# GpSimd issues its row scatters one by one, behind units of the cross attention and gates of expert blocks

## The chip, the cores and the metric

The kernel runs on one core of a Trainium2 chip. The metric is device time in microseconds; lower is better. The core has TensorE (PE, matrix products into PSUM), VectorE (DVE), ScalarE (ACT), GpSimd (POOL) and SyncE (SP), which run on their own and meet through semaphores, and 16 DMA engines that all queues share.

## What is computed

Two decoder layers on `x` (4 batches of 256 rows, 256 wide, float32), each with self attention, cross attention and a feed-forward part. The part around the change is the end of layer 1: its cross attention and its mixture of experts.

```python
x = x + _L1_attn_ref(_layernorm(x), w_qkv, b_qkv, w_out, b_out)
x = x + _L1_xattn_ref(_layernorm(x), ctx_512, Wq, Wkv_expand, Wout)      # 16 heads, causal, 256 x 256
x = x + _L1_ffn_ref(_layernorm(x), gate_weight, w_gate, w_up, w_down)
...
logits = x @ gate_weight.T                        # 28 experts
topk_w, topk_idx = jax.lax.top_k(softmax(logits), 6)
topk_w = topk_w / (topk_w.sum(-1, keepdims=True) + 1e-20)
# for every expert: h = silu(x @ wg) * (x @ wu);  y += w_tok * (h @ wd)     wg, wu: 256 x 176, wd: 176 x 256
```

## The kernel before, in words

Every engine works through a fixed list of pieces. `plan()` writes the lists; for layer 1 they are spelled out by hand in `ORDERS`, one string per engine, and a piece `sc.1.2` means the call `sc(1, 2)` in that engine's block. An engine executes its list strictly in order, and waits inside a piece stop everything behind it on that engine.

**Cross attention.** 32 units, `x` unit i being half of a head group of batch i // 8. For a unit TensorE makes the scores (`xs`), VectorE two negated maxima (L2026 and L2027, which count up semaphore `x_nm`), ScalarE the exponentials (L2556, L2557) in place of the scores, TensorE transposes them (`xt`, L851), ScalarE copies these back, and after every second unit comes the product with the values (`xpv`), which VectorE copies out (L2039). Three units are in flight, in three pairs of PSUM banks. Among the units lie the projections and the ends (`xe_...`) of each batch.

**Routing.** For batch b (256 rows): VectorE normalizes the rows (`rt_xh`, L2073; GpSimd does the power -0.5 for it, L2671), TensorE turns them and multiplies with the gate weights (`rt_tr`, `rt_g`), VectorE takes the maximum (L2080, semaphore `rt_m`), ScalarE the exponentials, VectorE the six best (`rt_k`), and `rt_p` gives each of the 256 x 6 row copies its place in the DRAM table `xg`, which has room for 1024 rows per expert (L2127 writes the places, semaphore `pos`). GpSimd then issues 12 indirect DMAs per batch: each takes 128 rows of 272 floats and scatters them to `xg` (L2738). These are the row scatters of this case. The places and rows are double buffered, so `rt_xh` of batch b waits for all 12 of batch b - 2.

**Block tables.** `mn`, `mc`, `ms` make, from the counts, tables of which half blocks (64 rows of one expert) come next. `ms.0` (after batches 0 and 1) fills expert pairs 0 to 4, `ms.1` pairs 5 to 10, `ms.2` the rest up to 30 (`FIRST = (0, 5, 11, NPAIR)`).

**Expert pairs.** There are 62 blocks of 128 rows (two half blocks each), in 31 pairs. SyncE's piece `ld(q)` loads the rows of pair q + 3 from `xg` (L784) and weights of pair q + 2 (L799). Where pair p starts a new table it waits first for all row scatters of the batches it rests on:

```python
if p in FIRST:
    for b in range(turn(p) + 2):
        e.wait_ge(sem(f"xg{b}"), 16 * 12)
```

The buffer of a block is free when the block 12 places before it has been scaled. ScalarE copies the block's expert weights (`wc`, L2278, `ws<-W_all`), TensorE transposes the rows (`et`), multiplies with gate and up weights (`eu`), ScalarE takes silu (L2632, semaphore `sg`), VectorE multiplies (L2216 to L2219), TensorE transposes (`eh`) and multiplies down (`ed`), VectorE scales the result with the routing weight (`ed`, L2240 and L2242), and GpSimd adds the 128 rows to one of two DRAM tables, `y0` or `y1`, with an indirect DMA that accumulates (`ed` of GpSimd, L2757). An add waits for the landing of the one before it on the same table, blocks alternate between the two, and VectorE has 10 result buffers. At the end SyncE reads the tables back and VectorE adds them to `x`.

GpSimd has, besides the scatters and adds, only small work in this part: the power steps (L2671) and a fill of zeros (`hm`).

Of the kernel before, what the change touches and what calls it, by code (L numbers as in the profile page):

```python
# [52 lines left out]
def half(h):  # L53
# [57 lines left out]
    "POOL": (  # L111
# [37 lines left out]
class Plan:  # L149
# [7 lines left out]
    def add(self, name, *args, banks=(), told=True, only=None):  # L157
        self.seq.append((name, args, only))
        mine = []
        for b in banks:  # L160
            mine.append((b, self.k[b], self.f[b]))
            if name != "w":
                self.k[b] += 1
                self.f[b] += told
        if only in (None, "PE"):
            self.fills[(name, *args)] = mine
# [18 lines left out]
def plan():  # L185
    p = Plan()
    add = p.add
# [142 lines left out]
    def experts():  # L330
        for q in range(5, NPAIR + 1):
            if q + 2 < NPAIR:
                add("ld", q)
            add("ed", q - 1, banks=[5, 6])
            if q < NPAIR:
                add("eh", q, banks=[4])
            if q + 2 < NPAIR:
                add("et", q + 2, banks=[q % 2])
            for j in (2 * q + 2, 2 * q + 3):
                if j < NB:  # L340
                    add("eu", j, banks=[2 + j % 2])
            if q + 2 < NPAIR:
                add("wc", q + 2)
        add("out")

    experts()
    return p


def program(nc, D):  # L350
    ctx = ExitStack()
    with ctx:
# [3 lines left out]
        def sem(name):  # L356
            if name not in sems:
                sems[name] = ctx.enter_context(nc.semaphore(name))
            return sems[name]
# [9 lines left out]
        def fills(name, *args):  # L369
            return [Fill(B[b], full[b], free[b], k, f) for b, k, f in P.fills[(name, *args)]]  # L370

        def fill(name, *args):
            return fills(name, *args)[0]
# [104 lines left out]
        at = bqkv_base  # L478
# [10 lines left out]
        at = fgu_base  # L489
        U = parts("U", 8, 256)  # L490
        at = r2_base + 4 * c2.at
# [5 lines left out]
        at = fwo_base + 4 * c3.at  # L497
        OT.append(parts("OT1", 256))
        assert at <= fwo_base + 4 * 4096
        at = fwd_base  # L500
# [50 lines left out]
        sg = [cm(176) for _ in range(2)]  # L551
# [58 lines left out]
        posi = [c1(12).bitcast(I32), pos2[:, :].bitcast(I32)]  # L610
# [230 lines left out]
        def _(e):  # L841
# [478 lines left out]
            def u_pv(i):  # L1320
                b, _, rh = unit(i)
                u = fill("upv", i)
                if i % 4 == 1:
                    w = fill("vtr", b, 1)
                    e.wait_ge(w.free, w.k + 1)
                for w in fills("ut", i - 1) + fills("ut", i):
                    e.wait_ge(w.free, w.k + 1)
                room(u)
                for r in range(4):
                    for j in range(4):  # L1330
                        a = mm(u.t[32 * j:32 * j + 32, r * 128:r * 128 + 128], va4[b % 2][:, 4 * rh + r, 32 * j:32 * j + 32],
                               PTu[slot_t("u", i - 1 + j // 2)][:, 4 * (j % 2) + r, :], True, True)
                a.then_inc(u.full, 1)
# [259 lines left out]
        def _(e):  # L1593
# [398 lines left out]
            def u_pv(i):  # L1992
                b, _, rh = unit(i)
                u = fill("upv", i)
                if b >= 2:
                    e.wait_ge(sem("scrw"), 16 * (b - 1))
                e.wait_ge(u.full, u.f + 1)
                o = O4[b % 2].rearrange("p (m x e) -> p e m x", m=4, e=2)[:, rh]
                e.tensor_copy(o, u.t[:, :].rearrange("p (m x) -> p m x", m=4)).then_inc(u.free, 1)
# [647 lines left out]
        def _(e):  # L2647
# [25 lines left out]
            def ln(tiles):  # L2673
                for t in tiles:
                    rstd((rs[:, t:t + 1], rs[:, t:t + 1]))
# [51 lines left out]
                e.tensor_tensor(Pu[m], Pu[m], rcu[m].rearrange("p (g o) -> p g o", o=1).to_broadcast([128, 8, 128]),  # L2727
                                ALU.mult).then_inc(sem("un"), 1)

            def sc(b, part):  # L2730
                xr = xrs[b % 2]
                if b == 0:
                    e.wait_ge(sem("init"), 16 * (NE + 1 + NY))
                e.wait_ge(sem("pos"), b + 1)
                e.wait_ge(sem("xr"), 3 * b + 3)
                e.wait_ge(sem("xh_rt"), 2 * b + 2)
                for i in range(3 * part, 3 * part + 3):
                    e.indirect_dma_start(out=D["xg"][:, :], out_offset=bass.IndirectOffsetOnAxis(ap=posi[b % 2][:, i:i + 1], axis=0),  # L2738
                                         in_=xr[:, i // 6, :], in_offset=None).then_inc(sem(f"xg{b}"), 16)


            def hm():
# [18 lines left out]
            def pair(b):  # L2761
# [3 lines left out]
                    "x0_bn": x0_bn,  # L2765
                    "x0_stat2": pair, "rest": rest, "rms1": lambda: rms(1), "rms2": lambda: rms(2),
                    "l1_stat": lambda t0, t1: ln(range(t0, t1)), "l1_init": l1_init, "un": un, "xp_stat": pair,
                    "rt_stat": pair, "sc": sc, "hm": hm, "ed": ed}
            for name, args, only in P.seq:
                if name in mine and only in (None, "POOL"):  # L2770
                    mine[name](*args)
# [119 lines left out]
```

## Time and profile before

| | |
|---|---|
| median of 3 runs | 814.88 us (807.21 to 815.64) |
| profiled execution, its own time | 808.85 us |
| its span, first to last instruction | 807.0 us |
| mean granted clock of TensorE | 0.916 |
| TensorE busy | 690.9 us, 86% |
| VectorE, ScalarE, GpSimd busy | 476.7, 376.4, 286.2 us |

The profile is one execution. Times count from the start of its span. A row of the timeline or of a line's group ends with the idle time of the engine before it and, after an arrow, what ended it; "issue" means nothing that the profile shows, "remote" a semaphore update from a source that it can't name.

### The profile page before, as it was taken

How to read it: one execution, taken by the hardware profiler on the slowest of the kernel's cores; microseconds unless marked ns; L12 is line 12 of the kernel's file. 1: busy time of each engine (PE TensorE's matmuls, PEld its weight loads, DVE VectorE, ACT ScalarE, POOL GpSimd, SP SyncE). 2: the span in 40 equal slices, each digit the busy share in tenths (PEclk: the TensorE clock that was granted, in tenths of full speed). 3: DMA queues.
4: the chain of work that ended last, by engine and by line, in shares of the span. 5: the costliest groups of instructions: out<-in, count | busy, mean ns of one | idle time of the engine just before them, and what ended most of it. 6: DMA issues, size and time to landing. Idle time of an engine off the chain costs nothing.

```text
span 807.0 us, 15683 instructions
## 1 busy us (share of the span) xinstructions
PE 690.9 (86%) x5129; PEld 472.3 (59%) x5136; DVE 476.7 (59%) x1413; ACT 376.4 (47%) x1026; POOL 286.2 (35%) x279
## 2 busy tenths in 40 slices
PE   8898999999879988798988999698648699999960
PEld 6666687777535766687756766466424355554530
DVE  2567669788867545546664756345425366665555
ACT  2464556555411502545657367436323256555520
POOL 3043544454410002212310402412445656566550
PEclk9999999999999999979997999858568799999985
DMA  8999999002150034313000019603334578778767
GB/s 330 296 349 350 349 348 379 7 1 76 59 215 18 0 124 126 113 37 105 27 28 1 1 31 404 239 22 145 103 114 103 104 129 148 144 143 148 135 106 235
DMA packets 86077, 116.89 MB, mean 145 GB/s; under 512 B 8364, under 2 KB 77293, under 8 KB 84974
## 3 DMA queue, kind: packets, MB, share of 16 engines
q1 hardware_dynamic: 70140, 97.71, 37.4%
q0 software_dynamic: 11168, 14.75, 10.7%
q10 hardware_dynamic: 4690, 3.43, 1.5%
q8 instruction: 43, 0.70, 0.4%
q14 instruction: 36, 0.29, 0.1%
HBM read 59.82 MB, written 56.04 MB: 144 GB/s over the span
## 4 chain that ended last, share of the span: by engine, by line
PE 35%; issue 5%; DVE 5%; another core or an unknown queue 3%; ACT 3%; DMA 2%; ACTq 1%; POOL 0%; SPq 0%; DVEq 0%; POOLq 0%
PE PS L843 28%; PE PS L851 8%; DMA y<-fwd 1%; ACTq L2609 1%; ACT ws L2278 1%; DVE few L1974 1%; ACT R L2496 1%; DMA W_all<-y 1%; DVE few L2027 0%; DMA y<-late,fwd 0%; DVE few L2026 0%; DVE R L1981 0%; DVE R L2102 0%; ACT R L2557 0%
## 5 line engine op out<-in xcount | busy, mean ns | idle before, releaser
L843 PE MATMUL PS<-R 32*128 32x128 f32 (+11 forms) x1048 | 138.1, 376 | 9.9 <-DVE R L2102 2.1
L843 PE MATMUL PS<-W_all,fgu 128*64 x372 | 113.7, 453 | 11.5 <-DVE fgu L2227 7.5
L843 PE MATMUL PS<-ws,fgu 128*64 128x352 f32 (+1 forms) x372 | 114.0, 454 | 0.0
L843 PEld LDWEIGHTS PS<-R 32*128 32x128 f32 (+5 forms) x1048 | 86.6, 196 | 43.5 <-issue 25.3
L2278 ACT ACTIVATE R<-PS 128x512 f32<-128x512 f32 (+5 forms) x136 | 67.6, 546 | 44.8 <-PE PS L851 31.9
L851 PE MATMUL PS<-ident,R 128*128 128x128 f32 (+1 forms) x504 | 75.7, 291 | 11.9 <-POOL R L2727 3.9
L843 PEld LDWEIGHTS PS<-W_all,fgu 128*64 128x64 f32 x372 | 49.4, 142 | 60.2 <-issue 27.5
L851 PEld LDWEIGHTS PS<-ident,R 128*128 128x128 f32 (+1 forms) x504 | 58.8, 150 | 33.6 <-issue 19.7
L2278 ACT ACTIVATE ws<-W_all 128x960 f32 x62 | 58.8, 996 | 25.3 <-issue 25.3
L2671 POOL TENSOR_TENSOR rs<-rs,mh 128x1 f32<-128x1 f32 x48 | 26.8, 561 | 111.5 <-DVE rs L1611 111.2
L2727 POOL TENSOR_TENSOR R<-R 128x1024 f32<-128x1024 f32 x16 | 30.3, 1900 | 100.1 <-DVE R L1983 100.1
L2681 POOL TENSOR_TENSOR R<-R 128x512 f32<-128x512 f32 x44 | 44.9, 1041 | 56.8 <-DVE R L1710 56.8
L2757 POOL DMA_INDIRECT y<-late,fwd x30 | 46.6, 1553 | 30.6 <-DVE late L2242 12.4
L2360 ACT ACTIVATE R<-PS,R 128x256 f32<-128x256 f32 x88 | 40.4, 473 | 28.9 <-DVE R L1702 28.9
L1695 DVE TENSOR_REDUCE R<-PS 128x2 f32<-128x512 f32 x64 | 41.1, 683 | 20.9 <-PE PS L843 20.5
L843 PEld LDWEIGHTS PS<-ws,fgu 128*64 128x64 f32 x372 | 49.4, 142 | 0.5 <-issue 0.5
L2757 POOL DMA_INDIRECT y<-fwd x20 | 31.3, 1565 | 40.1 <-DVE fwd L2242 20.4
L2632 ACT ACTIVATE fwd<-PS 128x176 f32<-128x176 f32 x62 | 19.5, 317 | 54.9 <-PE PS L843 26.1
L2496 ACT ACTIVATE R<-PS,few 128x128 f32<-128x128 f32 x128 | 34.6, 396 | 16.8 <-DVE few L1974 16.7
L843 PE MATMUL PS<-negm,identb 128*128 128x512 bf16 (+1 forms) x146 | 33.9, 343 | 4.4 <-DVE fwo L1758 1.6
L2278 ACT ACTIVATE xT<-PS 128x256 f32<-128x256 f32 (+1 forms) x32 | 13.4, 441 | 47.7 <-PE PS L851 44.3
L2026 DVE TENSOR_REDUCE few<-PS 128x2 f32<-128x256 f32 x32 | 13.5, 423 | 36.6 <-PE PS L843 26.4
(342 smaller groups left out, 1570.0 us busy)
## 6 DMA issues: line engine op xcount, KB each, us to landing
xg<-zrow SPq DMA_DIRECT2D x28, 1088.0 KB, 12.4
W_all<-in_wgu SPq DMA_DIRECT2D x2, 3360.0 KB
xh<-xg SPq DMA_DIRECT2D x74, 68.0 KB
y<-zrow SPq DMA_DIRECT2D x2, 2304.0 KB, 16.1
W_all<-in_wgu SPq DMA_DIRECT2D x1, 4320.0 KB
R<-in_wqkv SPq DMA_DIRECT2D x1, 4096.0 KB, 21.2
scrq<-bqkv SPq DMA_DIRECT2D x12, 256.0 KB, 2.9
R<-scrq SPq DMA_DIRECT2D x12, 256.0 KB, 3.0
```

Of the source, the lines that this page charges most:

```text
L843: return e.matmul(out, l, r, start=start, stop=stop, skip_group_check=True)
L851: return e.transpose(out, a, ident[:, :] if idt is None else idt)
L1695: own.mark(e.tensor_reduce(mx[s][:, :, hh], us[hh].t[:, :].rearrange("p (q k) -> p q k", q=2), X, ALU.max))
L2026: e.tensor_reduce(m[:, 0:2], PS[:, b0:b0 + 2, 0:128], X, ALU.max, negate=True).then_inc(sem("x_nm"), 1)
L2278: return e.activation(out, a, ACT.Copy)
L2360: a = e.activation(Pr[2 * (j % 3) + hh][:, qc, :], us[hh].t[:, qc * 256:qc * 256 + 256], ACT.Exp, bias=nb[s][:, qc, hh:hh + 1], scale=SA, ...
L2496: a = e.activation(Pu[m][:, g, :], us[jj].t[:, r * 128:r * 128 + 128], ACT.Exp, bias=mxx[m][:, g:g + 1], scale=1.0)
L2632: e.activation(sg[j % 2], u.t[:, 0:176], ACT.Silu).then_inc(sem("sg"), 1)
L2671: e.tensor_tensor(v[1], v[0], mh[:, 0:1], ALU.pow).then_inc(sem("rstd"), 1)
L2681: e.tensor_tensor(p, p, rc[j % 2][:, :, hh:hh + 1].to_broadcast([128, 2, 256]), ALU.mult).then_inc(sem("norm"), 1)
L2727: e.tensor_tensor(Pu[m], Pu[m], rcu[m].rearrange("p (g o) -> p g o", o=1).to_broadcast([128, 8, 128]), ALU.mult).then_inc(sem("un"), 1)
L2757: e.indirect_dma_start(out=D[f"y{y}"][0:to, :], out_offset=bass.IndirectOffsetOnAxis(ap=toi[j % NYS][rows, :], axis=0), in_=ys[j % NYS][ro ...
```

## The change

The piece `sc(b, part)` issued three scatters; now `sc(b, i)` issues one, and GpSimd's list holds 48 such pieces in place of 16. New pieces that only wait stand between them: `at(i)` waits until VectorE has taken the maxima of unit i, `top(b)` until it has taken the router's maxima of batch b, `pv(i)` until it has copied the value product of unit i, and `sg(j)` until ScalarE has the silu of block j. The adds of result rows (`ed`) keep their order and now lie between the scatters of batch 3, of which the last five are issued in the loop of the experts, behind pairs 4 to 6. The lists of the other engines are as they were.

```diff
--- before.py
+++ after.py
@@ -110,9 +110,11 @@
         "wc.4 et.5 eu.8 eu.9 wc.5 et.6 eu.10 eu.11 wc.6 "),
     "POOL": (
         "l1_stat.2.4 l1_stat.4.6 l1_stat.6.8 l1_init un.0 un.1 un.2 un.3 un.4 un.5 un.6 un.7 un.8 xp_stat.0 "
-        "un.9 un.10 xp_stat.1 un.11 un.12 un.13 xp_stat.2 un.14 rt_stat.0 un.15 xp_stat.3 sc.0.0 rt_stat.1 "
-        "sc.0.1 sc.0.2 sc.0.3 sc.1.0 rt_stat.2 sc.1.1 sc.1.2 sc.1.3 sc.2.0 sc.2.1 rt_stat.3 hm sc.2.2 sc.2.3 "
-        "ed.0 sc.3.0 sc.3.1 ed.1 sc.3.2 sc.3.3 ed.2 ed.3 "),
+        "un.9 un.10 xp_stat.1 un.11 un.12 un.13 xp_stat.2 un.14 rt_stat.0 un.15 xp_stat.3 at.17 sc.0.0 at.18 sc.0.1 at.19 sc.0.2 at.20 sc.0.3 rt_stat.1 at.21 sc.0.4 at.22 sc.0.5 at.23 "
+        "sc.0.6 sc.0.7 at.24 sc.0.8 sc.0.9 at.25 sc.0.10 sc.0.11 at.27 sc.1.0 at.28 sc.1.1 sc.1.2 at.29 sc.1.3 sc.1.4 "
+        "rt_stat.2 at.30 sc.1.5 sc.1.6 at.31 sc.1.7 sc.1.8 top.2 sc.1.9 sc.1.10 pv.31 sc.1.11 sc.2.0 sc.2.1 rt_stat.3 hm sg.0 sc.2.2 sc.2.3 "
+        "sg.1 sc.2.4 sc.2.5 sg.2 sc.2.6 sc.2.7 sg.3 sc.2.8 sc.2.9 sg.4 sc.2.10 sc.2.11 ed.0 sg.6 ed.1 sc.3.0 sg.7 sc.3.1 "
+        "sc.3.2 sg.8 sc.3.3 ed.2 sg.9 sc.3.4 sc.3.5 sg.10 sc.3.6 ed.3 "),
     "SP": (
         "a_wr.0.0 a_wr.0.1 a_wr.0.2 a_rd.0.0 a_wr.1.0 a_rd.0.1 a_rd.0.2 ld_m4 a_rd.1.0 a_wr.1.1 a_wr.1.2 "
         "a_rd.1.1 a_wr.2.0 a_rd.1.2 a_wr.2.1 a_wr.2.2 a_rd.2.0 a_rd.2.1 a_rd.2.2 a_out.0 a_wr.3.0 a_wr.3.1 "
@@ -332,6 +334,10 @@
             if q + 2 < NPAIR:
                 add("ld", q)
             add("ed", q - 1, banks=[5, 6])
+            if q < 8:
+                add("sg", 2 * q + 1, only="POOL")
+                for i in range(2 * q - 3, min(2 * q - 1, 12)):
+                    add("sc", 3, i, only="POOL")
             if q < NPAIR:
                 add("eh", q, banks=[4])
             if q + 2 < NPAIR:
@@ -2727,16 +2733,28 @@
                 e.tensor_tensor(Pu[m], Pu[m], rcu[m].rearrange("p (g o) -> p g o", o=1).to_broadcast([128, 8, 128]),
                                 ALU.mult).then_inc(sem("un"), 1)
 
-            def sc(b, part):
+            def at(i):
+                e.wait_ge(sem("x_nm"), 2 * i + 2)
+
+            def top(b):
+                e.wait_ge(sem("rt_m"), 2 * b + 2)
+
+            def pv(i):
+                u = fill("xpv", i)
+                e.wait_ge(u.free, u.k + 1)
+
+            def silu(j):
+                e.wait_ge(sem("sg"), j + 1)
+
+            def sc(b, i):
                 xr = xrs[b % 2]
                 if b == 0:
                     e.wait_ge(sem("init"), 16 * (NE + 1 + NY))
                 e.wait_ge(sem("pos"), b + 1)
                 e.wait_ge(sem("xr"), 3 * b + 3)
                 e.wait_ge(sem("xh_rt"), 2 * b + 2)
-                for i in range(3 * part, 3 * part + 3):
-                    e.indirect_dma_start(out=D["xg"][:, :], out_offset=bass.IndirectOffsetOnAxis(ap=posi[b % 2][:, i:i + 1], axis=0),
-                                         in_=xr[:, i // 6, :], in_offset=None).then_inc(sem(f"xg{b}"), 16)
+                e.indirect_dma_start(out=D["xg"][:, :], out_offset=bass.IndirectOffsetOnAxis(ap=posi[b % 2][:, i:i + 1], axis=0),
+                                     in_=xr[:, i // 6, :], in_offset=None).then_inc(sem(f"xg{b}"), 16)
 
 
             def hm():
@@ -2765,7 +2783,7 @@
                     "x0_bn": x0_bn,
                     "x0_stat2": pair, "rest": rest, "rms1": lambda: rms(1), "rms2": lambda: rms(2),
                     "l1_stat": lambda t0, t1: ln(range(t0, t1)), "l1_init": l1_init, "un": un, "xp_stat": pair,
-                    "rt_stat": pair, "sc": sc, "hm": hm, "ed": ed}
+                    "rt_stat": pair, "at": at, "top": top, "pv": pv, "sg": silu, "sc": sc, "hm": hm, "ed": ed}
             for name, args, only in P.seq:
                 if name in mine and only in (None, "POOL"):
                     mine[name](*args)
```

## Rows read from the trace of the kernel before

**Rows 1.** The page: TensorE's line, its granted clock in 40 slices, a DMA issue

```profile
PE 690.9 (86%) x5129; PEld 472.3 (59%) x5136; DVE 476.7 (59%) x1413; ACT 376.4 (47%) x1026; POOL 286.2 (35%) x279
...
PEclk9999999999999999979997999858568799999985
...
R<-scrq SPq DMA_DIRECT2D x12, 256.0 KB, 3.0
```

**Rows 2.** Windows: start and end, length, busy us (count) of engines, clock, DMA share

```profile
core 0: us, PE busy (x) PEld busy (x) DVE busy (x) ACT busy (x) POOL busy (x), PEclk, DMA share, GB/s
465.10:509.00 43.90, 41.65 (x383) 29.85 (x382) 26.22 (x75) 28.99 (x82) 4.81 (x6) 1.00 0.63 242
509.00:561.00 52.00, 45.65 (x320) 30.85 (x319) 22.92 (x80) 25.80 (x72) 14.49 (x17) 0.70 0.30 113
561.00:584.90 23.90, 14.43 (x78) 11.29 (x78) 10.44 (x42) 9.03 (x21) 10.99 (x12) 0.64 0.32 104
584.90:609.40 24.50, 14.35 (x88) 7.83 (x90) 6.72 (x37) 9.86 (x18) 9.34 (x13) 0.72 0.33 100
609.40:649.60 40.20, 29.35 (x170) 14.92 (x167) 19.70 (x88) 11.46 (x20) 24.23 (x20) 0.79 0.52 115
```

**Rows 3.** Timeline, VectorE: start, length, operation; units 21 and 31 open

```profile
509.01 0.43 DVE L2026 TENSOR_REDUCE few<-PS 128x2 f32<-128x256 f32 x1
...
560.98 0.42 DVE L2026 TENSOR_REDUCE few<-PS 128x2 f32<-128x256 f32 x1 [0.32 <-issue]
```

**Rows 4.** Groups by line, VectorE, 650 to 780 us: count, busy, mean ns

```profile
L2227 DVE COPY fgu<-PS 128x384 f32<-128x384 f32 x26 | 14.2, 547 | 0.0
```

**Rows 5.** Timeline, GpSimd: scatters at the ends of long runs

```profile
509.88 1.04 POOL L2738 DMA_INDIRECT xg<-R  x1 [0.25 <-issue]
...
569.67 0.96 POOL L2738 DMA_INDIRECT xg<-xr,pos  x1 [0.30 <-issue]
...
595.61 0.96 POOL L2738 DMA_INDIRECT xg<-R  x1 [0.30 <-issue]
...
616.48 0.99 POOL L2738 DMA_INDIRECT xg<-xr,pos  x1 [2.84 <-DVE pos L2127]
...
634.24 0.96 POOL L2738 DMA_INDIRECT xg<-xr,pos  x1 [0.30 <-issue]
```

**Rows 6.** The scatters' line: ns min/median/max, first and last start

```profile
L2738 POOL DMA_INDIRECT xg<-R x24: 956/960/1211, 490.7 to 595.6; - x24
```

**Rows 7.** Timeline, TensorE and VectorE, around the ends of the long runs

```profile
522.81 1.48 PE L843 MATMUL PS<-F,R 128*17 128x256 f32 x16 [6.25 <-issue]
...
572.47 0.28 DVE L2080 TENSOR_REDUCE R<-PS 128x1 f32<-128x28 f32 x2 [8.32 <-remote]
...
593.03 1.09 PE L851 MATMUL PS<-ident,xr 128*128 128x128 f32 x4 [5.27 <-issue]
599.01 0.87 PE L851 MATMUL PS<-ident,fwd 128*128 128x128 f32 x3 [4.89 <-issue]
...
623.59 0.66 PE L843 MATMUL PS<-SelT,fgu 48*64 48x256 f32 x8
...
635.31 0.21 DVE L2240 TENSOR_SCALAR fwd<-xh,R 128x1 int32<-128x1 f32 x1 [6.50 <-remote]
```

**Rows 8.** Windows: a short run of scatters, and the start of a long one

```profile
490.00:495.00 5.00, 4.97 (x50) 3.04 (x48) 2.89 (x7) 3.62 (x12) 3.15 (x3) 1.00 1.03 409
...
509.80:514.80 5.00, 5.00 (x47) 3.47 (x46) 1.30 (x4) 2.75 (x7) 3.92 (x4) 1.00 0.90 350
```

**Rows 9.** Timeline, GpSimd: two adds of result rows at the even pace

```profile
668.21 1.55 POOL L2757 DMA_INDIRECT y<-late,fwd  x1 [1.46 <-DMA y<-xq,fwd]
670.78 1.55 POOL L2757 DMA_INDIRECT y<-late,fwd  x1 [1.03 <-DVE late L2242]
```

**Rows 10.** Timeline: row loads of SyncE; TensorE turns rows of pair 11

```profile
573.51 6.25 SPq L784 DMA_DIRECT2D xh<-xg  x8
...
667.46 2.44 SPq L784 DMA_DIRECT2D xh<-xg  x4
...
669.91 0.38 PE L851 MATMUL PS<-ident,zrow 128*128 128x128 f32 x2
```

## Prediction

> **What bounds the kernel now.** I read the page first: TensorE is busy 86% of the span, but the line of granted clock shows that this is not one even stretch of work [rows 1]. In its slices 26 to 32 (20.2 us each, so 504 to 646 us) the clock is down to 5 to 8 tenths, while it is 9 in nearly all others. So I cut that part into stretches with the view of windows [rows 2]. The first stretch, 12 units of the cross attention (an operation of L2026 opens each unit on VectorE; the stretches begin and end with one, [rows 3]), runs at full clock. The next one has 10 units, yet takes 52.0 us; then come the end of the attention, the first expert blocks and four expert pairs, all at a mean clock of 0.64 to 0.79. From 650 us on TensorE sets the pace: 26 copies of an expert pair's activations in 130 us, 5.0 us a pair [rows 4].
>
> What sits in the slow part and nowhere else are GpSimd's row scatters. The timeline of GpSimd shows them in runs: one lasts 0.96 us and the next follows 0.30 us later, 1.26 us a piece [rows 5, 6]. There are four long runs: 9 scatters from 509.88 us, 9 up to 570.63 (a run of the second batch), 12 up to 596.57, with two pow steps and a fill of zeros among them, and 12 for the last batch from 616.48 to 635.20, with two result adds in the middle. The other engines' timelines show a hole at the end of each run [rows 7]: TensorE stands 6.25 us until 522.81, VectorE waits 8.32 us until 572.47 for gate matmuls, TensorE stands 5.27 us until 593.03 and 4.89 until 599.01. The best row is the last: TensorE issued the down products of pair 2 at 623.59 and was through by 624.25, and VectorE, which waits for nothing but them, scales them at 635.31, right after the last scatter of the run ended (635.20). The program names no cause ("remote"); what the rows show is that TensorE's word to the others arrives late while GpSimd issues indirect DMAs back to back, and that the lateness piles up with the length of the run. Short runs are free: with 3 scatters in 490 to 495, TensorE is busy 4.97 of 5.00 us; in 509.8 to 514.8, with the first 4 of a long run, 5.00 of 5.00; only then does it starve [rows 8]. The result adds are indirect DMAs too, 1.55 us each, two per pair, about 2.5 us apart [rows 9], in a phase at TensorE's own pace. So 0.6 of a GpSimd busy with them costs nothing when it pauses in between.
>
> **The change, part by part.**
> *Removed: the long runs.* I cost each stretch against what it would take without holes.
> (a) 509 to 561 us: 10 units in 52.0 us. The stretch before had 12 in 43.9, 3.66 us each [rows 2, 3], so 36.6; saved 15.4. Bounds: the hole alone, 6.2; and TensorE's own work at full clock, 45.65 us busy times the mean clock 0.70, 32 us, so 20. I take the units' rate, since both stretches carry the same kinds of side work. Most of it is clock: the mean is 0.70 here and 1.00 before.
> (b) 561 to 584.9: the wait of 8.32 us covers four transposes, one copy and eight matmuls, together near 2.3 us by their own lengths; saved 6 (0 to 8.3). Late next is ScalarE's chain (weight copies, table load), which starts from the same point, so it moves too.
> (c) 584.9 to 609.4: two holes of 5.27 and 4.89; some 2 us of them would stay as plain latency of the gates; saved 8 (5 to 10).
> (d) 609.4 to 649.6 (VectorE's scaling of pair 0 to that of pair 4): four pairs in 40.2 us. At 5.0 a pair [rows 4] that is 20, with 3 for the routing of batch 3 that lies among them (some 6 us of VectorE, partly beside TensorE); saved 17 (10 to 18).
> Sum removed: 46.4.
>
> *Moved: a scatter now stands behind a unit.* POOL's own order gets 16 units' waits, blocks' waits, one for the router's maximum and one for the last attention product. Each scatter also repeats three waits that are met already: sequencer time, which I put at 0 (at most the 0.30 us gap once more each, 48 x 0.3 = 14 us of GpSimd, not of TensorE). Queued behind these waits on GpSimd are the pow steps of batches 1 to 3's norms (0.55 us, VectorE waits for them) and the adds. The pow steps stand behind units that VectorE has passed anyway, so they are late by at most one pair of scatters, 2.5 us, beside attention units in flight: 0 taken. A single scatter can hold one hand-over of TensorE by up to 0.96 us. With 1 or 2 per 3.66 us unit and three units in flight I charge 1.5 us for (a) and 1 for (c) (bounds 0 and 0.96 x 24 = 23; rows 8 and 9 are nearest, and both show nothing).
>
> *Moved: rows become complete later.* Row loads of a pair wait for all 12 scatters of a batch. Batch 1: the last scatter is now behind the last attention product; in the profile that is 572.7, after it the router's maximum at 572.47 [rows 7]; both come 6 us sooner by (b), so the first row load is issued near 570.5 to 572.5 instead of 573.51 [rows 10]. It stands beside the chain of (b) and I charge 0 (up to 3). Batch 2: complete behind block 4's gates, its rows are used two pairs later: 0 (up to 2).
> Batch 3 is the one that costs. From the adds of pair 1 on GpSimd has 12 scatters and, up to the last of them (behind the adds of pair 6), 10 adds: 12 x 1.26 + 10 x (1.55 + 0.30) = 33.6 us without a pause. If pair 0 is scaled at T, the adds of pair 1 end near T + 11.7, so the last scatter ends at T + 45.3. From the end of a batch's last scatter to the first row load it took 573.51 - 570.63 = 2.9 us, four half-block loads take 2.44 us to issue [rows 10], and some 2.5 us to land (an estimate from 3.0 us for a 256 KB read on the page [rows 1]): T + 53. TensorE turns pair 11's rows at 669.91 now, 60.5 us after pair 0's scaling; less the 17 of (d), T + 43.5. So TensorE waits 9.5 us there, once; if it is slowed before by the same crowd, that comes out of the 9.5. Half clock after the hole: 0.5. Charge 10 (5 to 13).
>
> The 62 adds, the weights and everything after 680 stay. The end of the kernel hangs on the last adds' landings, which are as now.
>
> Sum: 46.4 - 1.5 - 1 - 10 = 34 us off a span of 807.0, 773, and with the 1.85 us around it 775 against the profiled 808.85. That execution is 6 us under the median of the three (814.88) and 1.6 over the lowest. The new kernel's median may lie as far above its own sum; I put the forecast at **776**.
>
> **A rule that speaks against it.** All 24 scatters of a kind take 0.956 to 1.211 us [rows 6], whatever VectorE does beside them. The Trainium skill (SBUF — State Buffer, the note on how VectorE blocks DMA) says that GpSimd cannot write descriptors while VectorE runs a two-port operation. It gives 0.62 us for a DMA alone and 3.1 beside such an operation, and spreading the scatters would then put more of them beside VectorE's work. By that rule and its figure, as an estimate, each scatter could cost up to 2.5 us more GpSimd time, 30 us in the crowded part of batch 3, and the result would be near 805; the trace does not agree, its longest is 1.21.
>
> **The rivals.**
> 1. *Tolls instead of holes, in part.* Each lone scatter delays a hand-over that somebody needs, and the blocks' gates are as dense as the scatters behind them (a block per 2.5 us, two scatters of 2.52). Half of the 46.4 stays: 808.85 - 23 + 10 = 796. For it: VectorE's and ScalarE's waits in the blocks are tight. Against: rows 8 and 9.
> 2. *The holes have another cause* (late instructions, or the DMA traffic that keeps the 16 engines 0.90 busy around 512 us [rows 8]) and only coincide with the runs. Then nothing moves but waits: 808 to 815. For it: the trace names no releaser. Against: four of four long runs have their hole, ended within 2 us of the run, and short runs have none.
> 3. *Slower: each lone scatter costs its whole 1.26 us on the path*, because GpSimd now waits for exactly the unit that the others wait for, so that it always issues when TensorE has something to say. 48 x 1.26 = 60 us against 46.4 removed, 14 slower: 823 (more with batch 3's wait). The point is a toll of 46.4 / 48 = 0.97 us per scatter. Against: the 3 scatters at 490 us.
> 4. *The port:* VectorE's operations stretch the scatters to some 3 us, late rows of batch 3 then eat the gain: 805, as a mechanism of 12 x 2.2 more before pair 11.
>
> **How the numbers follow.** Forecast 0.68 (its own range 764 to 789: all savings at 52 and charges at 8, or savings at 38 and charges at 18), rival 1 0.15, rival 2 0.08, rival 3 0.07, rival 4 0.02. The forecast's range and rival 1 give 0.8 between 762 and 803. A change of under 1% (8 us) can't be told from none here, since the three runs are 8.4 us apart. Faster by over 1% (under 806.7): 0.68 + 0.15 + 0.01 = 0.84. Same: 0.08. Slower: 0.08.
>
> **What would show it.** Right: granted clock near 1.00 from 509 to the start of the blocks, ten units in 37 to 39 us; no wait over 3 us of VectorE for the gate matmuls; no idle of 5 us of TensorE before pair 8; a stop of 5 to 10 us at pair 11's first transposes, with row loads issued just before and GpSimd busy without pause before that. Wrong: holes of the old size with scatters a unit apart (rival 2), units at 4.5 us or more each with full clock (1, 3), scatters over 1.3 us (4). The size would be off most easily at pair 11, where the order of 22 indirect DMAs decides, and in (a), if the clock drops for another reason.

## The result, and the profile after

The changed kernel takes 782.98 us (median of 4 runs, 781.5 to 788.41), the kernel before 812.54 in the same comparison (4 runs, 807.21 to 815.64). The ratio is 0.9646, its 95% interval 0.9596 to 0.9697: 3.5% faster. The forecast was 776.0 with a range of 762 to 803. The profiled execution took 783.2 us (span 781.3, mean clock 0.940), which is 25.7 us less span than before. Medians in this document are over all runs, while ratios and their intervals leave out the slow runs, over 1.5% above the fastest of their kernel (two of `late_table` and three of `late_table_spread`).

The page of the changed kernel, TensorE's line and its clock in 40 slices (19.5 us each), against [rows 1]:

```profile
PE 678.3 (87%) x5129; PEld 465.0 (60%) x5136; DVE 475.5 (61%) x1413; ACT 375.7 (48%) x1026; POOL 286.8 (37%) x279
...
PEclk9999999999999999988999799999589999999985
```

The dent of seven slices (the 26th to the 32nd before) has become one slice of 5 (547 to 566 us) and one of 8 (566 to 586); the lower slices ahead of it and at the end are there before the change too. To see what each stage gave I cut both traces at the same operations: units 9, 21 and 31 opening on VectorE (L2026 before, L2032 after), ScalarE's silu of block 0 (L2632, L2638), and VectorE's scaling of pairs 0, 4, 10 and 30 (L2242, L2248).

| stage | before | after | saved | forecast |
|---|---|---|---|---|
| start to unit 9 | 465.1 | 467.3 | -2.2 | 0 |
| units 9 to 21 | 43.9 | 43.3 | 0.6 | 0 |
| units 21 to 31 (a) | 52.0 | 36.4 | 15.6 | 13.9 |
| unit 31 to pair 0 (b, c) | 48.4 | 37.4 | 11.0 | 13 |
| pair 0 to pair 4 (d) | 40.2 | 30.3 | 9.9 | 17 |
| pair 4 to pair 10 | 30.2 | 39.8 | -9.6 | -10 |
| pair 10 to pair 30, and the end | 127.2 | 126.7 | 0.5 | 0 |

The windows of the changed kernel, from unit 9 on, answer to [rows 2]; the columns are those named there. The first row is the stretch of units 9 to 21, the second units 21 to 31, then to block 0's silu, to pair 0, to pair 4, and to pair 10.

```profile
467.30:510.70 43.40, 41.67 (x383) 29.90 (x383) 26.23 (x76) 28.89 (x82) 5.42 (x7) 1.00 0.62 239
510.70:547.10 36.40, 34.19 (x307) 23.28 (x309) 22.55 (x79) 25.22 (x72) 15.62 (x19) 0.96 0.46 176
547.10:571.30 24.20, 17.19 (x103) 12.69 (x95) 11.56 (x46) 11.06 (x23) 8.14 (x9) 0.63 0.30 94
571.30:584.50 13.20, 10.31 (x72) 5.54 (x71) 5.40 (x31) 7.42 (x14) 8.14 (x12) 0.91 0.47 142
584.50:614.80 30.30, 25.39 (x176) 12.59 (x175) 19.21 (x88) 12.19 (x20) 20.27 (x18) 0.95 0.57 133
614.80:654.60 39.80, 32.22 (x237) 16.76 (x236) 18.62 (x73) 17.06 (x29) 25.23 (x18) 0.94 0.67 130
```

In the second row GpSimd is busy as long as before (15.62 us against 14.49), yet TensorE works 34.19 of 36.40 us at a clock of 0.96, where it worked 45.65 of 52.00 at 0.70. The same work in fewer busy microseconds: about 11 us of the 15.6 are the clock (45.65 less 34.19), the other 4 are idle time of TensorE that is gone. The end of the attention (third row) is still at 0.63: it ends in real waits, of the projections' chain and the first expert rows.

The group of the scatters answers to [rows 6]: one for each of the two row buffers, ns min/median/max.

```profile
L2756 POOL DMA_INDIRECT xg<-R x24: 954/960/1191, 497.2 to 588.9; - x24
L2756 POOL DMA_INDIRECT xg<-xr,pos x24: 954/960/1036, 531.7 to 634.3; - x24
```

They cost what they cost before. The 3.1 us of the Trainium skill that the prediction weighed (SBUF — State Buffer, "A bandwidth-pool intuition that's wrong") is seen in no run here: spread out among VectorE's work, no scatter took over 1.191 us.

And this is where the experts' gain ends. VectorE's scalings of result rows in the timeline, of pairs 1 and 3, then TensorE's down products for them, and its stop:

```profile
593.39 0.21 DVE L2246 TENSOR_SCALAR fwd<-xh,R 128x1 int32<-128x1 f32 x1 [1.36 <-remote]
...
609.65 0.21 DVE L2246 TENSOR_SCALAR fwd<-xh,R 128x1 int32<-128x1 f32 x1 [5.42 <-remote]
```

```profile
590.38 0.66 PE L849 MATMUL PS<-SelT,fgu 48*64 48x256 f32 x8
...
601.89 0.66 PE L849 MATMUL PS<-xq,fgu 48*64 48x256 f32 x8
...
639.08 0.55 PE L857 MATMUL PS<-ident,fwd 128*128 128x128 f32 x3
642.82 0.41 PE L857 MATMUL PS<-ident,xT 128*128 128x128 f32 x2 [3.19 <-DMA xT<-xg]
```

The down products begun at 590.38 are picked up at 593.39. Those of pair 3, begun at 601.89 and through by 602.55, are picked up at 609.65: VectorE has waited 5.42 us for a source the program can't name, as in the last of [rows 7]. It is a lateness of the old kind, in a smaller size. The last row of TensorE is the stop at pair 11's rows. GpSimd's and SyncE's side of it:

```profile
621.61 0.99 POOL L2756 DMA_INDIRECT xg<-xr,pos  x1 [0.31 <-DMA y<-late,fwd]
622.90 0.97 POOL L2756 DMA_INDIRECT xg<-xr,pos  x1 [0.30 <-issue]
624.18 1.61 POOL L2775 DMA_INDIRECT y<-fwd  x1 [0.31 <-issue]
...
634.33 0.99 POOL L2756 DMA_INDIRECT xg<-xr,pos  x1 [0.30 <-issue]
```

```profile
637.95 1.14 SPq L790 DMA_DIRECT2D xT<-xg  x2
639.28 1.12 SPq L790 DMA_DIRECT2D zrow<-xg  x2
```

From 621.61 on these are nine indirect DMAs in a row (four are shown) with 0.30 us between them: scatters and adds have closed up to a long run again. Its last scatter ends at 635.32, SyncE issues the loads from 637.95, TensorE gets the rows at 642.82.

### The profile page after: what moved, and what is told of

It is laid out like the page before. It is cut to its first block, busy times and chain, and to the rows that moved or that the text cites. A ratio compares the mean times of both kernels' runs of the same rounds, so it can differ in the third digit from the quotient of the medians.

```text
span 781.3 us, 15742 instructions
## 1 busy us (share of the span) xinstructions
PE 678.3 (87%) x5129; PEld 465.0 (60%) x5136; DVE 475.5 (61%) x1413; ACT 375.7 (48%) x1026; POOL 286.8 (37%) x279
## 4 chain that ended last, share of the span: by engine, by line
PE 32%; DMA 5%; issue 4%; DVE 4%; ACT 3%; another core or an unknown queue 1%; POOL 1%; ACTq 1%; SPq 1%; POOLq 0%; DVEq 0%
PE PS L849 25%; PE PS L857 7%; DMA y<-fwd 2%; DMA y<-late,fwd 1%; ACTq L2615 1%; DMA xg<-xr,pos 1%; POOL y L2775 1%; DMA W_all<-y 1%; DVE few L1980 1%; ACT R L2502 1%; ACT ws L2284 1%; DMA xT<-xg 0%; POOL xg L2756 0%; DVE few L2033 0%
## 5 line engine op out<-in xcount | busy, mean ns | idle before, releaser
L849 PE MATMUL PS<-W_all,fgu 128*64 x372 | 110.7, 444 | 10.1 <-issue 3.7
L849 PE MATMUL PS<-ws,fgu 128*64 128x352 f32 (+1 forms) x372 | 111.0, 444 | 0.5 <-issue 0.5
L2733 POOL TENSOR_TENSOR R<-R 128x1024 f32<-128x1024 f32 x16 | 30.3, 1900 | 100.3 <-DVE R L1989 100.2
L849 PEld LDWEIGHTS PS<-ws,fgu 128*64 128x64 f32 x372 | 48.4, 138 | 1.7 <-issue 1.7
L2638 ACT ACTIVATE fwd<-PS 128x176 f32<-128x176 f32 x62 | 19.5, 317 | 46.4 <-PE PS L849 29.0
L2756 POOL DMA_INDIRECT xg<-R x24 | 23.6, 981 | 41.8 <-DVE few L2033 27.4
```

Source lines behind the costliest of these rows:

```text
L849: return e.matmul(out, l, r, start=start, stop=stop, skip_group_check=True)
L2638: e.activation(sg[j % 2], u.t[:, 0:176], ACT.Silu).then_inc(sem("sg"), 1)
```

## The experiments

My theory after the result: indirect DMAs issued back to back make TensorE's word to the others late, the lateness grows with the length of the run whatever it is made of, and the change took the runs apart in the attention but not among the experts, where scatters and adds together keep GpSimd full. Rivals: (B) the amount of DMA traffic or of GpSimd's work in a stage counts, not its spacing; (C) the whole experts part is only the late rows of batch 3.

The runs fell on three chips. Ratios are within one chip. Times of stages of the kernel before and of the changed kernel come from the two traces of the result, and which chip they ran on isn't known, so a comparison with them may be across chips. The times of the kernel before on the three chips were 814.96 (chip 1, 13 runs, 805.67 to 817.28), 812.81 (chip 2, one run) and 774.7 (chip 3, 17 runs, 771.38 to 781.75). That last number is a finding of its own.

**Each half of the change alone (chip 1).** `attn_only` has the new list up to the last scatter of batch 1, then the old order; `experts_only` the reverse.

```diff
 # attn_only: GpSimd's list from sc.1.11 on, and no scatters in the experts' loop
+ sc.2.0 ... sc.2.5 rt_stat.3 hm sc.2.6 ... sc.2.11 ed.0 sc.3.0 ... sc.3.5 ed.1 sc.3.6 ... sc.3.11 ed.2 ed.3
 # experts_only: xp_stat.3 sc.0.0 sc.0.1 sc.0.2 rt_stat.1 sc.0.3 ... sc.1.11, then as in the change
```

> The scatters of batches 0 and 1 stand one by one behind attention units as in the changed kernel; those of batches 2 and 3 are issued in the old order (12 of batch 2 with two pow steps among them, then six, two adds, six of batch 3). Theory (long runs make the holes): the attention's ten units take 36 to 38 us as in the changed kernel (36.4), the holes of 5 us after batch 2's run and in batch 3's zone are back. The change's gain before pair 0 in the expert part is kept only in its share of the attention; pairs 0 to 10 take 70 us in both kernels, so the whole is 790 to 797. Rival (the holes have nothing to do with the order on GpSimd): 808 to 815. Rival (the gain came from the expert part): over 800.

> The reverse: batches 0 and 1 in the old order (runs of 3, 9, 3, 9), batches 2 and 3 as in the changed kernel. Theory: the ten units take 50 to 53 us with a hole near 516, the wait for the router's maximum of batch 2 is over 6 us again; silu of block 0 to pair 0 takes 13 us as in the changed kernel instead of 18.6; whole 800 to 806. Rival (all of the gain lies in the attention): 808 to 812.

`attn_only`: 792.44 us (4 runs), ratio 0.9782 [0.9689, 0.9875]. `experts_only`: 803.99 us (10 runs), ratio 0.9896 [0.9852, 0.994]. The windows of units 21 to 31, of pairs 0 to 4 and of pairs 4 to 10, first in `attn_only`:

```profile
512.60:548.90 36.30, 34.11 (x307) 23.22 (x309) 22.63 (x80) 25.25 (x72) 15.67 (x18) 0.97 0.48 179
591.70:632.40 40.70, 31.50 (x179) 16.08 (x178) 19.60 (x89) 11.75 (x20) 24.25 (x20) 0.76 0.52 113
632.40:662.40 30.00, 29.47 (x234) 15.60 (x233) 18.63 (x72) 17.32 (x30) 18.63 (x12) 1.00 0.77 137
```

and in `experts_only`:

```profile
511.40:564.10 52.70, 45.70 (x320) 30.43 (x319) 22.84 (x80) 25.62 (x72) 14.50 (x17) 0.71 0.30 113
603.80:635.90 32.10, 28.18 (x197) 14.60 (x195) 19.11 (x89) 11.98 (x20) 21.07 (x17) 0.91 0.59 132
635.90:675.30 39.40, 31.00 (x214) 15.77 (x215) 18.39 (x72) 16.96 (x29) 24.07 (x18) 0.87 0.65 123
```

The ten units take 36.3 us with the new order and 52.7 with the old. From pair 0 to pair 10 it is 70.7 us in the old order and 71.5 in the new, so what the new order gains among the experts it gains ahead of pair 0, in the gates of the blocks beside batch 2's scatters: 39.7 us from unit 31 to pair 0 in `experts_only`, against 48.4 before. The attention's half has a share in that stretch too, which takes 42.8 us in `attn_only`.

**A run put back in, of DMAs or of arithmetic (chip 1, then chip 2).** The new order, with a run of 12 further scatters of batch 0's rows into a table of their own (`dump`), or with 24 power steps of one column, which take GpSimd about as long and issue no DMA.

```diff
+ # run_dma, run_pow:   at.19 sc.0.2  xtra.0 ... xtra.11   at.20
+ # run_dma2, run_pow2: rt_stat.1     xtra.0 ... xtra.11   at.21
+ def xtra(i):                                     # run_dma, run_dma2 (waits and semaphore not shown)
+     e.indirect_dma_start(out=D["dump"][:, :], out_offset=..., in_=xrs[0][:, i // 6, :], in_offset=None)
+ def xtra(i):                                     # run_pow, run_pow2: two of
+     e.tensor_tensor(spare[:, k:k + 1], ones[:, k:k + 1], mh[:, 0:1], ALU.pow)
```

> The changed kernel with 12 more row scatters in one run without a pause, behind the third scatter of batch 0 (unit 19 of the attention). They write batch 0's rows once more, to a DRAM table that nobody reads. Theory: TensorE starves after five or six of them, a hole of 5 us or more and half clock after it, the ten units take 46 to 54 us instead of 36.4, whole 793 to 801. Rival (a run only coincides with something else near 516 us): units within 1 us, whole 782 to 785.

> The changed kernel with GpSimd kept busy at the same place by arithmetic: 24 powers of 128 numbers (0.55 us each, 13 us and more) in one run in place of the 12 extra scatters, with nobody waiting for them. Theory (it is the indirect DMAs): no hole, the units take 36 to 39 us, whole 782 to 786. Rival (a busy GpSimd is enough, because somebody waits for it): like the run of scatters, 793 or more.

`run_dma` 811.86 us, `run_pow` 797.26, one run each, both far above what was expected. Both made a hole: I had put the run ahead of batch 1's own power steps, for which VectorE waits, and that wait makes a hole whatever the run consists of (8.29 us in `run_pow`). Still the DMAs cost more than the arithmetic: units 9 to 31 take 104.8 us in `run_dma` and 87.9 in `run_pow`, and in `run_dma` VectorE waits 12.71 us for a unit's scores (L2027 at 526.33, "remote"). The second pair is the clean one; it has the run behind those steps.

> As run_dma, but the run of 12 extra scatters stands behind the pow steps of batch 1's norm (behind unit 20), so that no other engine waits for anything that GpSimd has behind the run, except batch 0's later scatters. In run_dma and run_pow those pow steps stood behind the run and VectorE waited for them. Theory (lateness of TensorE's hand-overs in long runs of indirect DMAs): still a hole of 5 us or more near 520 and half clock after it, the ten units take 46 us or more instead of 36.4. Rival (all of run_dma's loss was VectorE's wait for the pow steps): ten units in 37 to 39 us.

> As run_pow, 24 powers in one run, moved behind the pow steps of batch 1's norm as well. Theory: nobody waits for GpSimd, arithmetic does not hold TensorE's hand-overs, ten units in 36 to 39 us, whole 782 to 786. Rival (any busy GpSimd delays others): 44 us or more for the ten units, whole over 790.

`run_dma2` took 805.42 us and its units 21 to 31 57.7 us; `run_pow2` 789.32 and 43.8 (one run each). The windows of 5 us, first of `run_dma2` (the run lasts from 510.16 to 525.15, and two of batch 0's own scatters follow at once, to 527.68):

```profile
510.00:515.00 5.00, 4.96 (x47) 3.34 (x46) 1.23 (x4) 2.73 (x8) 3.93 (x4) 1.00 1.03 405
515.00:520.00 5.00, 1.52 (x15) 0.89 (x12) 0.57 (x2) 0.81 (x2) 3.78 (x5) 0.90 0.39 147
520.00:525.00 5.00, 0.62 (x8) 0.38 (x12) 0.46 (x1) 1.86 (x6) 3.78 (x5) 0.50 0.31 113
525.00:530.00 5.00, 3.77 (x25) 2.68 (x17) 0.00 (x0) 0.37 (x2) 2.07 (x3) 0.50 0.22 84
```

and of `run_pow2` (power steps from 510.19 to 524.37):

```profile
510.00:515.00 5.00, 5.00 (x48) 3.58 (x47) 1.66 (x5) 3.68 (x10) 4.69 (x10) 1.00 0.93 368
515.00:520.00 5.00, 4.90 (x55) 3.48 (x53) 2.45 (x7) 4.39 (x15) 4.69 (x9) 1.00 0.04 16
520.00:525.00 5.00, 5.00 (x49) 3.36 (x46) 4.41 (x20) 3.05 (x12) 4.48 (x9) 1.00 0.01 3
525.00:530.00 5.00, 4.52 (x39) 3.17 (x37) 3.35 (x10) 2.12 (x6) 3.78 (x5) 1.00 0.22 84
530.00:535.00 5.00, 2.45 (x22) 1.66 (x22) 1.36 (x4) 3.48 (x10) 3.81 (x4) 0.79 0.30 111
```

Beside 14 us of arithmetic TensorE is busy 14.90 of 15 us; beside the run of scatters 2.14 of the 10 us from 515 on, and a VectorE maximum that waits for it comes 9.62 us late (L2027 at 530.07, "remote"). So on this chip the run of indirect DMAs does it, a busy GpSimd does not. Rival B's traffic doesn't either: the 16 DMA engines are 0.93 busy from 510 to 515 in `run_pow2` with TensorE at 5.00 of 5 us, and 0.31 in `run_dma2` from 520 on, where TensorE starves. Nor does the amount: the ten units have 14 scatters beside them before the change and 14 after, and only their spacing differs. The time of `run_pow2` was missed: 782 to 786 and no hole were expected. The last row shows where it is. While GpSimd did arithmetic the units it was to wait for went by, so from 524.66 on nine scatters followed each other 0.30 us apart, a catch-up run, and made a hole of their own.

**Batch 3's scatters left out (chip 2).** Neither kernel scatters batch 3's rows or waits for them; the pairs do the same work on what the table holds. `no3_after` has the new order, `no3_before` the old.

```diff
-                e.indirect_dma_start(out=D["xg"][:, :], ...)
+                if b < 3:
+                    e.indirect_dma_start(out=D["xg"][:, :], ...)
...
-                        for b in range(turn(p) + 2):
+                        for b in range(min(turn(p) + 2, 3)):
```

> The changed kernel without the 12 scatters of batch 3 (its rows never reach the table, pair 11 waits for three batches only; the experts then work on empty rows in their place, at the same cost). It prices those 12 scatters where the change has put them. Theory (crowded GpSimd plus late rows cost the expert pairs their pace): pairs 0 to 10 take 53 to 57 us instead of 70.1, whole 766 to 770. Rival (TensorE's own work and the routing chain take the 70 us): 66 us or more, whole 779 or more.

> The kernel before without the 12 scatters of batch 3, likewise. Theory: pairs 0 to 10 take 53 to 57 us instead of 70.4, whole 790 to 794 against the profiled 808.85; the same price as in the changed kernel, which would explain why spreading them moved these pairs by 0.3 us only. Rival: the price here is higher or lower than after by over 4 us.

771.38 and 792.26 us, one run each (expected 766 to 770 and 790 to 794). The windows of pairs 0 to 4 and 4 to 10, of `no3_after`, then of `no3_before`:

```profile
583.20:607.50 24.30, 23.04 (x176) 11.90 (x175) 19.59 (x88) 12.33 (x20) 13.96 (x11) 0.97 0.60 117
607.50:638.40 30.90, 29.69 (x235) 15.62 (x233) 18.68 (x72) 17.00 (x30) 19.52 (x13) 1.00 0.79 147
```

```profile
608.10:634.70 26.60, 24.54 (x171) 12.88 (x168) 19.65 (x89) 11.84 (x20) 12.53 (x8) 0.87 0.57 103
634.70:664.70 30.00, 29.38 (x234) 15.50 (x233) 18.67 (x72) 16.64 (x30) 18.69 (x12) 1.00 0.77 142
```

Pair 0 to pair 10 takes 55.2 and 56.6 us without the 12 scatters, against 70.1 and 70.4 with them. So they cost 14 to 15 us in either order (if the result's chip is another one than chip 2, their times for the kernel before agree within 0.5%): in this stretch the change moved the cost and did not lower it. Over the whole kernel it is less in the new order, since `no3_after` takes 131.2 us behind pair 10 and the changed kernel 126.7. Leaving the scatters out shortens the runs and lowers the amount of work at once, so among the experts the two aren't told apart. Rival C is weakened too: of 14.9 us in the new order, pairs 0 to 4 carry 6.0, where no wait for batch 3's rows lies.

**A run of another kind of DMA, and extra scatters spread out (chip 3).** `run_plain2` has the run of `run_dma2` as ordinary DMAs of the same rows; `spread_dma` has the 12 extra scatters one by one, each behind one of batch 0's.

```diff
+ def xtra(i):                                     # run_plain2, placed as in run_dma2
+     e.dma_start(D["dump"][128 * i:128 * i + 128, :], xrs[0][:, i // 6, :])
+ # spread_dma, xtra of run_dma:  at.17 sc.0.0 xtra.0 at.18 sc.0.1 xtra.1 ...
```

> The changed kernel with 12 plain DMAs of the same rows and size (128 x 1088 B, to a DRAM table that nobody reads) from GpSimd's queue, in one run at the place of run_dma2. Theory A (whatever GpSimd writes descriptors for, back to back, holds TensorE's hand-overs): a hole near 520, ten units in 46 us or more. Theory B (only indirect DMAs, with their 128 row descriptors worked out one by one, do): ten units in 36 to 40 us.

> The changed kernel with the same 12 extra scatters spread: one directly behind each scatter of batch 0, so that runs are 2 to 4 long with units between them. Theory (only long runs hurt, a lone scatter is free): ten units in 36 to 39 us, whole 782 to 787, against 57.7 us and 805 with the same 12 in one run. Rival (each scatter has its toll of 0.5 to 1 us on the path): 42 to 48 us and 788 to 795.

779.44 and 780.47 us, one run each; units 21 to 31 take 34.0 us in both. First that window of `run_plain2`, then two of 5 us of `spread_dma` and three rows of its GpSimd:

```profile
515.20:549.20 34.00, 33.44 (x320) 23.18 (x319) 22.64 (x80) 24.97 (x72) 22.13 (x30) 1.00 0.64 238
```

```profile
525.00:530.00 5.00, 5.00 (x50) 3.32 (x47) 4.29 (x20) 3.17 (x12) 4.08 (x4) 1.00 0.31 115
530.00:535.00 5.00, 4.64 (x40) 3.29 (x38) 4.59 (x14) 3.15 (x10) 3.78 (x5) 1.00 0.30 111
```

```profile
521.22 0.95 POOL L2751 DMA_INDIRECT xg<-R  x1 [2.00 <-DVE few L2028]
522.48 0.96 POOL L2759 DMA_INDIRECT dump<-R  x1 [0.30 <-issue]
...
544.25 0.96 POOL L2751 DMA_INDIRECT xg<-xr,pos  x1 [0.30 <-issue]
```

No hole in either, but neither says what was asked of it. In `spread_dma` the scatters didn't stay spread: GpSimd fell behind the units, the waits passed at once, and from 521.22 to 545.21 us 19 scatters follow each other 0.30 us apart. On chip 2 a run of 14 left TensorE 2.14 of 10 us busy; here a run of 19 leaves it 5.00 and 4.64 of 5. So this chip isn't like the others: a long run of indirect DMAs costs nothing in the attention, spacing can't be tested here, and plain DMAs can't be told from indirect ones. The rest agrees: the kernel before takes 774.7 us, 38 less, and pairs 0 to 4 take 24.4 us (`run_plain2`) and 23.6 in the new order, scatters included, as they take elsewhere with batch 3's left out (24.3).

What they also show is the other cost by itself. TensorE's stop for pair 11's rows, first of `run_plain2`, then of `spread_dma` (the arrow names nothing here; the rows' loads stand just before it on SyncE's queue, as above):

```profile
639.01 0.66 PE L852 MATMUL PS<-ident,xT 128*128 128x128 f32 x2 [10.80 <-issue]
```

```profile
638.89 0.66 PE L852 MATMUL PS<-ident,xT 128*128 128x128 f32 x2 [12.08 <-issue]
```

The last scatter ends at 632.1, the loads are issued from 634.2, and TensorE, which comes on time here, stands 10.8 to 12.1 us. Pairs 4 to 10 take 43.7 and 44.8 us.

**The rows of batch 3 wanted later (chip 3).** The second table may fill pairs 5 to 12 instead of 5 to 10, so that the wait for batch 3 comes at pair 13. With these inputs batches 0 to 2 have enough blocks for 13 pairs; by the kernel's bounds only 11 are sure, and other inputs would get padding there. `late_table_spread` also puts batch 3's scatters one block further apart.

```diff
-FIRST = (0, 5, 11, NPAIR)
+FIRST = (0, 5, 13, NPAIR)
 # late_table_spread, besides:
+ ed.0 sg.6 ed.1 sc.3.0 sg.7 sc.3.1 sg.8 sc.3.2 ed.2 sg.9 sc.3.3 sg.10 sc.3.4 ed.3
+            if q < 10:
+                add("sg", 2 * q + 1, only="POOL")
+                for i in ((5, 6), (7,), (8, 9), (10,), (11,))[q - 5]:
```

> The changed kernel with the last block table starting at pair 13 in place of 11 (FIRST = (0, 5, 13, NPAIR)), nothing else. Pairs 11 and 12 then take rows of batches 0 to 2, so that batch 3's rows are needed two pairs later. Theory: TensorE's wait for the row loads at pair 11 (3.2 us and some half clock after it) is gone, pairs 0 to 10 take 65 to 67 us instead of 70.1, whole 777 to 780. Rival: the crowd of GpSimd's DMAs sets that pace by itself and the wait was only where the lateness showed: 782 to 784.

> As late_table, and batch 3's 12 scatters spread over pairs 1 to 9, one or two per pair, instead of pairs 1 to 6. GpSimd's indirect DMAs then take 5.3 us per pair of 5.0 instead of 6.2 and more. Theory: pairs 0 to 10 take 58 to 63 us, whole 769 to 776. Rival (adds and scatters together cost what they cost, wherever they lie): as late_table.

`late_table`: 768.78 us (8 runs, 766.49 to 783.73), 0.989 [0.9852, 0.9928] of the kernel before on this chip. `late_table_spread`: 775.38 (median of 10 runs, of which one took 1566.73 us for a reason that I don't know), 0.9988 [0.9949, 1.0028]. The windows of `late_table` from pair 0 to 4, to 10 and to 30:

```profile
580.70:605.10 24.40, 21.71 (x172) 11.30 (x168) 19.71 (x89) 11.87 (x20) 17.56 (x15) 1.00 0.67 147
605.10:635.40 30.30, 29.25 (x232) 15.38 (x230) 18.66 (x73) 16.76 (x29) 22.68 (x17) 1.00 0.79 167
635.40:740.80 105.40, 97.96 (x755) 50.79 (x753) 61.60 (x237) 56.47 (x94) 65.74 (x43) 0.98 0.75 135
```

The stop is gone, 13.4 to 14.5 us of it; 3 to 4 come back later, in single pairs of 5.5 to 6.5 us instead of 5.0. In the two late-table kernels pairs 0 to 10 take 54.7 and 55.4 us, less than expected; the expectations rested on traces of the slower kind of chip. Against `run_plain2` and `spread_dma`, which have the change's table, the median of `late_table` is 11 us lower; those are single runs with 12 more DMAs each, and two runs of `late_table` itself took 779 and 784, so the windows say this more safely than the times. The further spacing brings the stop back, since its last scatter ends at 634.99 instead of 629.58 (`late_table_spread`, TensorE at pair 13's rows):

```profile
642.50 1.09 PE L852 MATMUL PS<-ident,xh 128*128 128x128 f32 x4 [7.95 <-issue]
```

The changed kernel itself was not run on chip 3. With everything but the extra DMAs the same, `run_plain2` and `spread_dma` put it near 779 to 780, against 774.7 before: there the change would bring nothing or cost 0.6 to 0.7% (an estimate from two single runs, which lie within the 771.38 to 781.75 of the kernel before).

## Why the prediction was right, and where not

It was right in sign and range and 7 us optimistic (776 against 783). Of the 34 us net, 25.7 came.

- **(a)** Forecast 13.9, measured 15.6, in the change and in `attn_only` alike. The mechanism holds on the chips of the result and of `run_dma2`, which puts a run back and takes 57.7 us there. That the size came out so well is in part luck. The prediction took 36.6 us for ten units without holes and added 1.5; on chip 3, where nothing is late, the ten units take 34.0. If that is what they need, some 2.4 us were left where 1.5 were charged, and the rate was 2.6 too slow.
- **(b), (c)** Forecast 13 together, measured 11.0. The wait for the gates fell from 8.32 to 3.57 us, where the prediction wanted none over 3, the clock at the end of the attention stayed at 0.63, and the hand-overs of the first blocks stayed a little late.
- **(d)** This is the term that was mis-sized: 17 forecast, 9.9 measured, 30.3 us left for four pairs instead of 23.2. About 1 us of the 7 is the floor: even without batch 3's scatters four pairs take 24.3. The other 6 are the lateness. I had taken all runs as removed. Among the experts they were not, since the adds of [rows 9] are indirect DMAs too. From 587.55 to 637.2 us GpSimd issues 14 scatters and 15 adds with no pause over 1.84 us, and pairs 1, 3 and 6 take 9.1, 12.2 and 7.4 us instead of 5. The prediction had noted the 33.6 us "without a pause" and used it only for the rows' completion, not for the lateness that a run brings. The size lies between the forecast and rival 1, but not by rival 1's mechanism, a toll for each lone scatter. That it is the length of these runs, and not the amount of GpSimd's work here, is argued from the attention and not shown.
- **Batch 3's rows** Forecast a charge of 10, measured 9.6 between pairs 4 and 10, but by another split: the pairs themselves are 4.6 us late, and the stop is 5.1, of which 3.19 us idle and the rest a stretch at half clock (TensorE's products take 0.79 us instead of 0.46 from 643.6 to 646.6). The chain was mis-sized by a few microseconds at each end. With pair 0 scaled at T = 584.5, the last scatter ended at T + 50.8, not T + 45.3, and the rows were there at T + 58.3, not T + 53; TensorE wanted them at T + 55.1, not T + 43.5, because it had been slowed by the same crowd, as the prediction allowed. On chip 3, where it isn't slowed, it stands 10.8 to 12.1 us, a little above the 9.5 that was worked out for that case.
- **Rival 2** (another cause for the holes) and **rival 3** (each lone scatter costs 1.26 us) fall with the ten units at 36.4 us, 14 scatters beside them and a clock of 0.96. **Rival 4** falls with 1.191 us as the longest scatter.
- Two readings of the prediction were off without moving its sum. TensorE's second hole beside batch 2's run lasts to 599.01, 2.4 us past the end of the run (596.57) and not within 2; and GpSimd's new list waits for 14 units, not 16.
- The 2.2 us lost before unit 9 are not explained; over all traces this start takes 465.1 to 471.9 us, so it is within what it varies by.

What stays open: how a run of indirect DMAs delays TensorE's word, whether a run of ordinary DMAs would too, and why one chip of those used doesn't show it. I can say what the runs bound it to (not arithmetic, not the load of the DMA engines, and only when four or five stand in a row) and not what it is.

## What to carry to other kernels

When a queue engine issues indirect DMAs, look at how many follow each other without a pause, all kinds counted together, and not only at the ones that you move; and try it on more than one chip before you call it a gain. Spreading a batch of transfers delays its last one, so before you spread, look for who waits for all of it; here the later deadline (`late_table`, about 11 us on one chip, and only safe for inputs like these) was worth more than the further spacing, which took 7 us of it back. And a wait that paces a queue paces it only while the queue is on time: once held up, it releases everything it has passed in one run (nine scatters in `run_pow2`, 19 in `spread_dma`), which is just what the waits were to prevent.

## What the runs showed of the hardware that was not expected

- The same kernel takes 812 to 815 us on two chips and 774.7 on a third, 5% less. Its trace there was not taken, but the kernels with the new order show what is other on that chip: the ten units take 34.0 us at a clock of 1.00, even beside 19 scatters in a row, and pairs 0 to 4 take no longer than elsewhere without batch 3's scatters. A gain of 3.5% on one chip can be none on another.
- On chip 2 a run of 12 scatters more leaves TensorE 0.62 of 5 us busy in its last third. The ten units take 57.7 us against 36.4 in the trace of the result, 21 more, although the run itself lasts 15. TensorE's clock is 0.50 of full, its level of 1.2 GHz, from 520 us to 550, and 1.00 again only from 555, 27 us after the last scatter that follows on the run (527.68).
- Twenty-four power steps of one column, 14.18 us of GpSimd, leave TensorE idle for 0.10 us beside them (`run_pow2`).
